# A graph-and-FFN kernel on one Trainium2 core: the rails stage's prologue, with x transposed and loaded in two halves and the first unit written out

## The reference, cut to what matters

```python
xr = x.reshape(b, t, RAILS, RAIL_W)                    # x normalised; 64 rails of 16
y = jnp.einsum('btri,hrij->bthrj', xr, rail_maker)     # 4 heads
z = jnp.einsum('bthrj,hrkj->bthrk', y, rail_up_proj)
h = jax.nn.gelu(z.reshape(b, t, -1), approximate=False)
out = h @ w_cproj.T                                    # 16384 hidden columns to 1024
```

## Time and profile before

| | us |
|---|---|
| runs: median (lowest to highest), 3 runs | 2764.19 (2762.47 to 2764.22) |
| the profiled execution: its own time | 2761.69 |
| its span in the profile | 2760.0 |
| busy in the span: PE, VectorE, ScalarE, GpSimd | 2609.7, 1883.5, 1111.9, 125.4 |

### The profile page before, as it was taken

The page is one execution under the profiler, slowest core; times in us unless marked ns, Lnnn a source line. Parts: engine busy times, 40 slices in busy tenths (PEclk is TensorE's granted clock), DMA queues, the critical chain, the costliest instruction groups (busy, mean ns, idle before and its releaser), DMA issues. The chain is left out here.

```text
span 2760.0 us, 33800 instructions
## 1 busy us (share of the span) xinstructions
PE 2609.7 (95%) x12298; PEld 1726.0 (63%) x12298; DVE 1883.5 (68%) x2337; ACT 1111.9 (40%) x1148; POOL 125.4 (5%) x140
## 2 busy tenths in 40 slices
PE   8999469959999999999999999999999999989998
PEld 5555258836666666666666666666665565675776
DVE  7775768858887987888888789878877543223111
ACT  3211256645555455455545555554552221010111
POOL 0000000010000000000000000000000000000122
PEclk9999779959999999999999999999999999999999
DMA  5200400052223223222322232132320001025896
GB/s 159 62 28 30 89 0 1 1 163 68 60 53 90 53 53 74 68 61 52 90 68 60 53 88 54 42 85 68 85 81 1 14 0 33 31 83 186 291 337 194
DMA packets 172593, 214.58 MB, mean 78 GB/s; under 512 B 66426, under 2 KB 116220, under 8 KB 172458
## 3 DMA queue, kind: packets, MB, share of 16 engines
q1 hardware_dynamic: 166022, 197.24, 26.0%
q0 software_dynamic: 4896, 10.25, 1.5%
q10 hardware_dynamic: 1540, 5.12, 0.5%
HBM read 183.44 MB, written 32.52 MB: 78 GB/s over the span
## 5 line engine op out<-in xcount | busy, mean ns | idle before, releaser
L1453 PE MATMUL rails_ps<-keep_own_w1g,rails_hid_hi 128*125 128x512 f16 x2120 | 632.4, 380 | 2.2 <-issue 2.2
L1453 PE MATMUL rails_ps<-keep_own_w,rails_hid_hi 128*125 128x512 f16 x2080 | 618.7, 379 | 0.0
L1453 PE MATMUL rails_ps<-keep_own_w1g,rails_hid_lo 128*125 128x512 f16 x1060 | 402.5, 380 | 0.0
L1453 PE MATMUL rails_ps<-keep_own_w,rails_hid_lo 128*125 128x512 f16 x1040 | 394.2, 379 | 0.0
L1453 PEld LDWEIGHTS rails_ps<-keep_own_w1g,rails_hid_hi 128*125 128x125 f16 x2120 | 285.4, 137 | 159.1 <-DVE keep_X L1248 4.9
L1453 PEld LDWEIGHTS rails_ps<-keep_own_w,rails_hid_hi 128*125 128x125 f16 x2080 | 279.8, 137 | 151.3
L1002 ACT ACTIVATE rails_hid_hi<-rails_raw_a,keep_scale_hidden 128x1000 f16<-128x1000 f32 x210 | 274.8, 1334 | 210.7 <-DVE rails_raw_a L1213 96.2
L1194 DVE SCALAR_TENSOR_TENSOR rails_hid_lo<-rails_raw_a,keep_scale_hidden,rails_hid_hi 128x1000 f16<-128x1000 f32 x210 | 312.1, 1515 | 39.4 <-ACT rails_hid_hi L1002 39.4
L992 ACT ACTIVATE rails_raw_a<-rails_ps,keep_scale_gelu 128x1000 f32<-128x1000 f32 (+1 forms) x192 | 182.6, 953 | 349.0 <-PE rails_ps L1438 345.9
L1248 DVE SCALAR_TENSOR_TENSOR keep_X<-rails_ps,rails_out_scale,keep_X 125x1024 f32<-125x1024 f32 x180 | 198.6, 1103 | 144.9 <-PE rails_ps L1453 144.9
L1453 PEld LDWEIGHTS rails_ps<-keep_own_w1g,rails_hid_lo 128*125 128x125 f16 x1060 | 145.0, 137 | 84.4 <-issue 0.6
(11 more groups left out here) (327 smaller groups left out, 3523.7 us busy)
## 6 DMA issues: line engine op xcount, KB each, us to landing
carried_w_land<-cproj SPq DMA_DIRECT2D x79, 1024.0 KB
ffn_w<-W SPq DMA_DIRECT2D x51, 1024.0 KB, 12.4
rails_xs<-xt_d SPq DMA_DIRECT2D x128, 78.1 KB, 5.2
xt_d<-rails_acc SPq DMA_DIRECT2D x20, 250.0 KB
keep_X<-x SPq DMA_DIRECT2D x10, 448.0 KB
z_d<-open_z SPq DMA_DIRECT2D x10, 448.0 KB
att_zh<-z_d SPq DMA_DIRECT2D x4, 1120.0 KB
xn_d<-ffn_xn SPq DMA_DIRECT2D x10, 448.0 KB
```

The source lines that it names most:

```text
L1453: mm = nc.tensor.matmul(ps[0:P, t, :], hid[(q + b) % 2][l][:, k, t * P:(t + 1) * P], w[(q + b) % 2][r][:, k, :], start=(k == 0 and i == 0) ...
```

## The change

1. x comes back in halves. After the stores of tiles 0 to 4 SP waits until these have landed and loads the first half of pair 0's x (`x_half(0)`), and only then stores tiles 5 to 9; then `x_half(1)`, pair 1's x, and the bias row last. Loads of the first comb and the first half count on a semaphore of their own, `first_in`.
2. Turns 5 to 9 use banks 0 to 3 only, which leaves banks 5 to 7 to the hidden pieces.
3. The hidden pieces of a11 surround turn 9; those of a21 and a22 stand between the blocks of product 0 of unit 0.
4. ScalarE and VectorE make w_hi and w_lo of product 0 before copy 9, w_hi and w_lo of product 1 before the gelus of a21 and before s3, and ScalarE makes the gelus of a22 inside unit 0, after a_hi of product 1.
5. `over_units`: unit 0 is written out, units 1 to 12 are a loop of six rounds, units 13 and 14 are written out.

```diff
+        def turn_bank(t):
+            return 2 * (t % 4) if t < HALF_T else 2 * ((t - HALF_T) % 2)
...
         def over_units(eng, body):
-            with eng.Fori(0, END // 2) as i:
-                body(2 * i, 0, 2)
+            body(0, 0, 2)
+            with eng.Fori(0, END // 2 - 1) as i:
                 body(2 * i + 1, 1, 2)
+                body(2 * i + 2, 0, 2)
+            body(END - 2, 1, 2)
             body(END - 1, 0, 1)
...
+                def x_half(half, done):
+                    for q in range(4):
+                        sp.dma_start(xs[0][32 * q:32 * q + 32, half * WN:(half + 1) * WN].rearrange("p (t f) -> p t f", t=HALF_T),
+                                     xt_d[q % 2, 0:32, half * HALF_T:(half + 1) * HALF_T, 0:P]).then_inc(done, 16)
...
-                comb_load(0, 0, 0)
+                comb_load(0, 0, 0, first_in)
                 comb_load(1, 0, 1)
-                for t in range(TILES):
+                for t in range(HALF_T):
                     x_store(t)
-                sp.dma_start(row[:], bias.partition_broadcast(128)).then_inc(row_in, 16)
+                for k in range(STAGES):
+                    sp.wait_ge(stored[k], 32)
+                x_half(0, first_in)
+                for t in range(HALF_T, TILES):
+                    x_store(t)
                 for k in range(STAGES):
                     sp.wait_ge(stored[k], 32 * TILES // STAGES)
-                x_load(0, 0, 0)
+                x_half(1, xs_in[0])
                 x_load(1, 0, 1)
+                sp.dma_start(row[:], bias.partition_broadcast(128)).then_inc(row_in, 16)
...
# ScalarE
-                for t in range(TILES):
+                for t in range(TILES - 1):
                     x_hi(t)
...
+                w_hi(0, 0, 0)
                 gelu("a11", 0, 0, None, None)
                 gelu("a11", 1, 0, None, None)
+                x_hi(TILES - 1)
                 a_hi(0, 0, 0, 0)
                 gelu("a11", 2, 0, None, None)
                 a_hi(0, 0, 0, 1)
-                w_hi(0, 0, 0)
+                w_hi(0, 1, 0)
                 for j in range(3):
                     gelu("a21", j, 3, None, None)
-                for j in range(3):
-                    gelu("a22", j, 6, None, None)
...
                             a_hi(u, q + 1, b, 1)
-                            w_hi(u, q + 1, b)
+                            if isinstance(u, int) and u == 0 and q == 0:
+                                for j in range(3):
+                                    gelu("a22", j, 6, None, None)
+                            else:
+                                w_hi(u, q + 1, b)
...
# VectorE
-                for t in range(TILES):
+                for t in range(TILES - 1):
                     x_lo(t)
                     if t + 2 < TILES:
                         normalise(t + 2)
+                    if t == 7:
+                        scale_of(0, 0)
+                w_lo(0, 0, 0)
+                x_lo(TILES - 1)
+                a_lo(0, 0, 0, 0)
+                t3(0)
+                a_lo(0, 0, 0, 1)
+                scale_of(1, 0)
                 dve.wait_ge(xn_set, TILES)
                 nc.vector.tensor_tensor(quarter_of(0, 1), quarter_of(0, 1), quarter_of(1, 1), ALU.subtract)
-                scale_of(0, 0)
-                t3(0)
-                a_lo(0, 0, 0, 0)
-                a_lo(0, 0, 0, 1)
-                w_lo(0, 0, 0)
+                w_lo(0, 1, 0)
                 s3(0)
-                scale_of(1, 0)
                 dve.wait_ge(blank, 1)
...
                         take(u, q, 0, 2)
-                        if q < 6:
+                        if isinstance(u, int) and u == 0 and q == 0:
+                            pass
+                        elif q < 6:
                             w_lo(u, q + 1, b)
...
# TensorE
-                    if t >= 4:
-                        pe.wait_ge(xt_lo_set, t - 3)
+                    if t == 4:
+                        pe.wait_ge(xt_lo_set, 1)
+                    if t >= HALF_T:
+                        pe.wait_ge(xt_lo_set, max(HALF_T, t - 1))
...
+                def hidden_first(t):
+                    if t == 0:
+                        pe.wait_ge(xs_in[0], 64)
+                        hidden("a21", 0, ("a11", 0), 0)
+                        hidden("a21", 1, ("a11", 0), 0)
+                    if t == 1:
+                        hidden("a21", 2, ("a11", 0), 0)
+                    if t == 2:
+                        pe.wait_ge(xs_in[1], 128)
+                        hidden("a22", 0, ("a21", 0), 0)
+                        hidden("a22", 1, ("a21", 0), 0)
+                    if t == 3:
+                        hidden("a22", 2, ("a21", 0), 0)
+
-                for t in range(TILES):
+                for t in range(TILES - 1):
                     turn(t)
+                pe.wait_ge(first_in, 128)
+                hidden("a11", 0, None, 0)
+                hidden("a11", 1, None, 0)
+                turn(TILES - 1)
+                hidden("a11", 2, None, 0)
                 pe.wait_ge(xt_lo_set, TILES)
...
```

More of the change, by code:

```diff
@@ L809, in rails @@
         xs_in, w_in = [c.sem(f"xs_in{k}") for k in range(2)], {n: c.sem(f"{n}_in") for n in AT}
+        first_in = c.sem("first_in")
         stored = [c.sem(f"xt_stored{k}") for k in range(STAGES)]
@@ L828, in rails @@
         act_tick, pool_tick = c.sem("act_tick"), c.sem("pool_tick")
+        def turn_bank(t):
+            return 2 * (t % 4) if t < HALF_T else 2 * ((t - HALF_T) % 2)
         def turned(t):
-            return ps[:, 2 * (t % 4):2 * (t % 4) + 2, 0:4 * P].rearrange("p a (b f) -> p a b f", f=P)
+            return ps[:, turn_bank(t):turn_bank(t) + 2, 0:4 * P].rearrange("p a (b f) -> p a b f", f=P)
         def by_four(tile):
@@ L871, in x_store, with comb_load @@
                     sp.dma_start(xt_d[1, :, t], stage[t % STAGES]["lo"].rearrange("p o f -> p (o f)")).then_inc(stored[t % STAGES], 16)
-                def comb_load(b, octet, quarter):
+                def comb_load(b, octet, quarter, done=None):
                     rows = slice(quarter * 32, quarter * 32 + 32)
@@ L876, in comb_load @@
                         part = "lo" if q >= 2 else "hi"
-                        sp.dma_start(cm[b][32 * q:32 * q + 32, :, :], combs[part][rows, octet, :, :]).then_inc(xs_in[b], 16)
+                        sp.dma_start(cm[b][32 * q:32 * q + 32, :, :], combs[part][rows, octet, :, :])\
+                          .then_inc(xs_in[b] if done is None else done, 16)
+                def x_half(half, done):
+                    for q in range(4):
+                        sp.dma_start(xs[0][32 * q:32 * q + 32, half * WN:(half + 1) * WN].rearrange("p (t f) -> p t f", t=HALF_T),
+                                     xt_d[q % 2, 0:32, half * HALF_T:(half + 1) * HALF_T, 0:P]).then_inc(done, 16)
                 def x_load(b, octet, quarter):
@@ L915, in body @@
                     if left == 1:
-                        sp.wait_ge(xs_in[0], 128 * UNITS)
+                        sp.wait_ge(xs_in[0], 128 * UNITS - 64)
                         sp.wait_ge(xs_in[1], 128 * UNITS)
@@ L1419, in turn @@
                     pe.wait_ge(xn_set, t + 1)
-                    if t >= 4:
-                        pe.wait_ge(xt_lo_set, t - 3)
+                    if t == 4:
+                        pe.wait_ge(xt_lo_set, 1)
+                    if t >= HALF_T:
+                        pe.wait_ge(xt_lo_set, max(HALF_T, t - 1))
                     for k in range(KT):
-                        mm = nc.tensor.transpose(ps[:, 2 * (t % 4) + k // 4, (k % 4) * P:(k % 4 + 1) * P],
+                        mm = nc.tensor.transpose(ps[:, turn_bank(t) + k // 4, (k % 4) * P:(k % 4 + 1) * P],
                                                  xn[t % 2][:, k * 128:(k + 1) * 128], ident[0:P, 0:P])
@@ L1456, in project @@
                     mm.then_inc(acc_sum, 1)
-                for t in range(TILES):
-                    turn(t)
-                pe.wait_ge(xt_lo_set, TILES)
-                pe.wait_ge(xs_in[0], 128)
-                for j in range(3):
-                    hidden("a11", j, None, 0)
-                for j in range(3):
-                    hidden("a21", j, ("a11", 0), 0)
-                pe.wait_ge(xs_in[1], 128)
-                for j in range(3):
-                    hidden("a22", j, ("a21", 0), 0)
+                def hidden_first(t):
[12 more added lines that the diff above has]
+                for t in range(TILES - 1):
+                    turn(t)
+                pe.wait_ge(first_in, 128)
[3 more added lines that the diff above has]
+                hidden("a11", 2, None, 0)
+                pe.wait_ge(xt_lo_set, TILES)
                 def body(u, b, left):
@@ L1473, in body @@
                             project(u, q, b, t)
+                            if isinstance(u, int) and u == 0 and q == 0:
+                                hidden_first(t)
                             if t not in (0, 1, 3):
@@ L1480, in body @@
```

(2 more changed lines are left out.)

## The result

The changed kernel takes **2749.03 us** in the median of 6 runs (2747.79 to 2750.15); six runs of the kernel before on the same chip gave 2764.32 (2762.47 to 2764.66). The profiled execution of after has a time of its own of 2748.82 and a span of 2747.1, so by spans the saving is 12.9 us.

A forecast was written before the change was run, and what follows sets the result against it. PE was taken as the bound inside the loop, so only an earlier first product could save: its end moves from 632.52 to 621.3, 11.2 us, and 2764.2 - 11.2 = 2753.0 us. Range 2751 to 2758.

The forecast's parts named there:

- VectorE's margin at w_lo of the fifth product: Slack before PE wants the fifth product's split weights: from some 3.4 us to about 1, not turning negative.
- the price of the new loads: Half loads of x taken at the old loads' price: issued 0.64 us apart, each landing 3.0 after issue.
- first rendezvous: After five turns SP waits for their ten stores, until 589.1, then loads half of x, back at 594.0.
- the second: Second rendezvous: last store landed at 601.9, then x_half(1) loaded, back 4.9 us later at 606.8.
- (a): Rival, product 0: PE's gaps delay the clock's rise or drop it; saving 7 to 9, 2756 us; chance 0.18.
- (b): Rival, both rendezvous: stores drain late or reads land late, 5.2 instead of 3.0; saving 7, 2757 us; chance 0.12.
- (c): Rival, products two to five: VectorE becomes the bound, 1 to 2 us lost; saving 9.7, 2754.5 us; chance 0.12.
- (d): Rival: loads at the stage's worst, 10.2, at both rendezvous; 3 us slower than before, 2767 us; chance 0.03.
- (e): Rival: an unseen wait, from SP's order or the written-out units' code, takes back all; 2764 us; chance 0.05.

The follow-up runs named there:

- Slow halves: The changed kernel with four more 40 KB loads ahead of each half load of x, making each half 1.8 us later; 2749.42 us, ratio 0.9954.
- w1 late: The changed kernel with product 1's weights split after its a_hi and a_lo again, and the gelus of a22 ahead of unit 0; 2756.66 us, ratio 0.9976.
- warm: The changed kernel with fifteen matmuls that feed nothing filling PE's 3.45 us gap before product 0; 2749.66 us, ratio 0.9951.
- take early again: The kernel of take early, unchanged, measured once more beside the changed kernel; 2745.70 us, ratio 0.9944.
- loop-only: The kernel before with only the new units' loop: first and last unit of the old loop written out, six rounds instead of seven; 2762.58 us, ratio 0.9995.
- take early: The changed kernel with two gelus of a22 ahead of product 1's a_hi and unit 0's first take ahead of both a_lo; 2747.19 us, ratio 0.9941.

## Why the prediction was right and wrong

The sign and the mechanism were right, link by link; the forecast saving was too small by 2 us in the trace and by 4 in the medians.

| step | forecast | measured |
|---|---|---|
| stores of tiles 0 to 4 told, x_half(0) issued | 589.1 | 588.77 |
| its four loads: issue apart; landing | 0.64; 3.0 | 0.44; about 2 |
| hidden a11 starts | 594.0 | 592.18 |
| turn 9 done; gelus done | 597.2; 596.8 | 594.98; 596.49 |
| a_lo done, product 0 starts | 600.7 | 600.03 |
| last store issued; told | 599.4; 601.9 | 598.63; 600.70 |
| x_half(1) back | 606.8 | about 604.0 |
| block 0 ends; PE waits for x | 605.5; 1.3 | 604.98; none |
| s3 ends | 614.6 | 612.75 |
| PE waits for gelu of a22 | 2.0 | 1.85 |
| product 1 starts | 621.3 | 619.5 |
| VectorE's margin at w_lo of the fifth product | about 1 | 1.8 |

**The step that failed** is the price of the new loads: "The new loads carry half the bytes in runs of the same 250 bytes; I take the old price, the nearest row." The old price, 0.64 apart and 3.0 to land, belongs to loads of 78 KB; a half load measured 0.44 and 2.0. At the first rendezvous the error is 1.8 us (594.0 to 592.18; 1.5 from the loads, 0.3 because SP was released earlier), of which the next link, w_hi and the gelus on ScalarE, swallowed most: product 0 started only 0.7 earlier. At the second the load came back 2.8 earlier than forecast, 0.8 of it from the earlier x_lo 9, 0.4 from the store, 1.6 from the loads; the wait of 1.3 fell away, block 0 having ended 0.5 earlier as well. From there to product 1 every link kept its length: 606.8 to 621.3 is 14.5 us, and 604.98 to 619.5 is 14.5. Slow halves put the price back and got the forecast's dates back. The rows could have warned: issue took 0.61 us for a load of 78 KB and 0.32 for a store of 250 KB, so it does not follow bytes alone; that it stays when a load is halved was a choice without a row. What in a load sets its issue and landing was not tested.

The half loads of `x_half(1)` landed in 1.8 to 2.0 us and the full ones behind them in 2.0 to 3.7, 2.9 in the median. The Trainium skill, DMA: Bandwidth & Descriptors (Anatomy of one DMA), has a fit of 2.0 us plus bytes over 436 GB/s, made on another issuing path; worked out from it, as an estimate, 40 KB take 2.1 us and 78 KB 2.2. For the half loads the trace agrees nearly, and the fit did better than the row; for the full loads it is too low in the median, as the earlier trace rows had said.

**The rest of the miss** is a slip and the scatter. The slip: 632.52, from which 621.3 was taken, is the start of product 0's last matmul; product 1 started at 632.73, so the same working gives 11.4. The trace's own saving is 12.9 us by spans, 13.3 in the stage: 11.4 and the 1.9 of the loads. The scatter: three pairs of medians gave 15.3, 13.6 and 12.3, and the medians of all runs, 65 of before and 15 of the change, are 2763.36 and 2749.51, which is 13.9. So 13 to 14 us is what the change brings, the 15.3 has 1.5 to 2 us of scatter in it, and the range, which bore unknown costs alone, had no room for scatter. The loads alone put the forecast near 2751, at the low end of the range; that the time came 2 us below it is scatter, as far as the runs show.

**The rivals.** (a) The clock: it rose during turn 9 already and fell again in the 3.45 us gap; the second rise came between 604.7 and 604.8, at the end of block 0, and it stayed. The windows of after:

```profile
594.00:595.00 1.00, 0.97 (x7) 0.74 (x5) 0.30 (x2) 1.00 (x2) 0.00 (x0) 0.74 1.00 374
598.00:599.00 1.00, 0.00 (x0) 0.00 (x0) 1.00 (x2) 1.00 (x2) 0.00 (x0) 0.50 0.67 256
...
604.00:605.00 1.00, 1.00 (x5) 0.48 (x4) 0.98 (x3) 0.60 (x1) 1.00 (x1) 0.62 0.67 132
605.00:606.00 1.00, 1.00 (x11) 0.86 (x10) 1.00 (x1) 1.00 (x1) 1.00 (x1) 1.00 0.62 118
```

The rival did not come true, but w1 late and warm show its mechanism in this very product: there the clock fell in a wait of 6.32 us and just behind one of 2.29; in after it fell in the one of 3.45 and not in the one of 1.85. The Trainium skill, TensorE: Matmul & The Clock Gate (HAM oscillation), says that waits between bursts drop the array's clock, so that the next burst starts cold; the traces agree for the first three of these waits. (b) Late loads: the reverse happened. (c) VectorE as the bound: not in after, at 0.19 us in take early again. (d) and (e) did not come true; the loop-only run shows no cost of the written-out units, which was one of (e)'s two reasons.

## What to carry to other kernels

Interleaving the work that the first product does not need was worth more here (7.4 us, taken away last) than the early read and all the rest together (5.9), though the long wait for the read, 9.98 us, is what the profile showed first. Before removing one stall at the end of a product, follow the other engines to the same point: here ScalarE and VectorE came due within about 1 us of each other; moving the one gave 0.3 us, moving both 1.9. And where a transfer is cut in half, price it anew: neither its issue nor its landing need be that of the whole.

## What the runs showed of the hardware that was not expected

- Cutting a load in half cut its issue and its landing: in runs of 250 bytes, 40 KB were issued 0.44 us apart and landed in 2.0, 78 KB 0.64 apart and landed in 2.9 to 3.0, all in the median. Single loads stray: in warm one half load took 1.51 us of issue, and the landings of that execution's half loads went up to 3.0.
- Equal waits do not have equal effects on the clock. The 3.10 us wait in the last unit is the same in every trace; in after the granted clock over 2116 to 2120 was 0.61 and the unit took 109.7 us, in slow halves and both take-early traces the clock stayed up and the unit took 108.3, in warm it took 111.2. The code of that unit is the same in all. But each kernel that was traced more than once stayed on its side (before twice 110.0, after 109.7 to 110.0 three times, take early twice 108.3), so whether chance decides it or what ran before is open.
- The first turn starts anywhere from 567.6 to 569.9 in identical code, and what follows the last unit took 601.1 to 603.3 us. With the last unit's jumps these seem to be what spreads the executions of one kernel over 2 to 6 us; that they account for all of it was not shown.
- Keeping the array busy is no gain in itself: filler matmuls kept the clock up over one gap, PE then waited 2.29 us for a load, and the clock fell just behind that (warm, 1.5 us lost in the stage in one execution, with the slow load issue in it).
